# Second attention layer's keys: two batches prepared on VectorE alone in the layer before, two turned and split by GpSimd during the attention

## The chip, the cores and the metric

The kernel runs on one core of a Trainium2 chip. The metric is the device time in microseconds. Before the change three runs took 4261.15, 4261.16 and 4271.19 us, median 4261.16. The engines are named as in the profile: PE (TensorE), PEld (its weight loads), DVE (VectorE), ACT (ScalarE), POOL (GpSimd) and SP (SyncE, which here only issues DMAs).

## The reference

The network has four layers. Each adds a gated cross-attention and a gated feed-forward to x, [4 batches, 512 tokens, 256 features], float32. The context has 1601 rows of 256 features in each batch and is the same for all layers. The part that matters is the attention of the second layer, which turns (rotary position embedding) its queries and keys:

```python
q = (query @ Wq + bq).reshape(B, Sq, H, D)      # H = 16 heads, D = 16
k = (key @ Wk + bk).reshape(B, Sk, H, D)        # Sk = 1601
q = q * cq + _rotate_half(q) * sq_
k = k * ck + _rotate_half(k) * sk_
scores = einsum('bhqd,bkhd->bhqk', q, k) / sqrt(D)
scores = where(mask == 0, -1e+30, scores)
ctx = einsum('bhqk,bkhd->bqhd', softmax(scores), v).reshape(B, Sq, E)
```

In the first layer the attention is followed by a quantised linear map: x is layer-normalised, rotated by a Hadamard matrix, rounded to 4-bit levels and multiplied with a ternary weight.

## The kernel before

The stages run one after the other, with a fence between them: attention 1, quantised linear (926 to 1174 us of the span), attention 2 (1174 to about 2005 us), then experts, attention 3, experts, attention 4, experts. The context doesn't depend on x, so keys and values of an attention are prepared ahead, in the feed-forward stage in front of it, by the class `Prepared` and the functions `prepare_*`.

**Keys in parts.** In the first three attentions the scores are made of bfloat16 matmuls. A float32 key is split into three bfloat16 parts (`split3`, L873): part = value, rest = value - part, and so on. For the turned keys of attention 2 a piece (128 of the 256 key features x up to 512 of the 1601 context rows) goes through these steps in the quantised stage:

- PE makes the keys in PSUM (L267), ACT adds the bias and writes `p_kf` (L294).
- ACT issues two DMAs that copy `p_kf` with its two halves swapped into `p_kr` (L302).
- POOL or DVE does seven instructions (`prepare_split`, L335 to L337 and L876 to L879): p_kf x cosine, p_kr x sine, their sum, and the four of `split3`.
- SP stores the three parts to DRAM as `kready` (L239). ACT may overwrite a buffer of the ring of four only when this store has landed (the wait in front of L294).

Each of the four batches has the context chunks 512, 512, 512 and 65 rows wide. Two pieces a chunk make 32 pieces. With a chunk's keys PE also makes its values (L275), ACT copies them (L312) and stores them. The list in `quantised_linear` says which chunks belong to which of 11 parts and whether "pool", or "pool" and "dve" in turn, split them. The order of work is written by hand: `quant_pe`, `quant_act`, `quant_dve`, `quant_pool` place part by part between the layer norm "n", the four groups of tiles (`rotated`: x times the Hadamard matrix, L1603; `quantised` on DVE, L1550 to L1559; `xq` on POOL, L1505 and L1506; `product`, L1613 and L1622; the update of x on DVE, L1571) and the layer norm "c" (L95 to L145). Part 0 stands before norm "n", part 1 behind it, part 10 behind norm "c".

**Attention 2.** `Plan.lay_out_ready` writes a list of units that every engine runs through in order. `attend(g, b)` is one of 16 groups (four groups of four heads in four batches). It has 52 score steps `s2`, 0 to 51, and among them other units at steps given as (number, first, last): the row maxima of a later group (PE L1079, DVE L972, 988 ns each), then `peak` (DVE, six instructions on 128x16 numbers, L983 to L879), `turn` (PE L1085, DVE L991, then three DMAs `qaug<-tm`, L869, without which the next group's scores can't start), the softmax's `sum` and `norm`, and in `attend(0, b)` the two query pieces `q` of batch b+1, turned and split by POOL (L895 to L899 and L876 to L879). In `attend(1, b)` and later the `fetch` units load batch b+1's queries and keys (L844, L851) once the last scores of the old ones are done. SP issues its DMAs in the order of the units and waits in place.

PE runs through the same list. At the start of attention 2 SP issues weights, the table `turn`, the first keys, then after the two query pieces their fetch, output weights, values (L800), the keys of groups 1 to 3, and then the first `qaug<-tm` (L869).

## Time and profile before

| what | us |
|---|---|
| median of three runs | 4261.16 |
| the profiled execution, its own time | 4263.7 |
| its span, first to last instruction | 4262.5 |
| PE busy | 3602.4 (85%) |
| DVE busy | 2254.9 (53%) |
| ACT busy | 2084.6 (49%) |
| POOL busy | 641.6 (15%) |

The page gives for each group of instructions the busy time, the mean of one, and the idle time in front of it with what ended it. PE's weight loads overlap its matmuls. A granted clock of 1.00 is 2.4 GHz, of 0.50 is 1.2 GHz. The chain that ended last is only three pieces long here (12 us of the last expert stage), so it says nothing about the stages that are changed. They are read by windows and in order of time.

### The profile page before, as it was taken

The numbers are of one execution on the slowest core, as the hardware profiler recorded it, in microseconds if no ns is written. First come the engines' busy times: TensorE is split into PE (matmuls) and PEld (weight loads), VectorE is DVE, ScalarE is ACT, GpSimd is POOL, SyncE is SP. The second block draws the span as 40 slices with busy tenths as digits, with TensorE's granted clock in tenths as the row PEclk, the third lists the DMA queues.
The fourth block names the chain that finished last, engine by engine and source line by source line (L and its number), as shares of the span: only waits on it lengthen the run. The fifth ranks groups of instructions, "written<-read, shape, count | busy, mean of one in ns | idle before, by whom it ended". The sixth has DMA issues, their size and how long they took to land. (4 is left out here: it accounts for less than half of the span.)

```text
span 4262.5 us, 54212 instructions
## 1 busy us (share of the span) xinstructions
PE 3602.4 (85%) x19494; PEld 1931.4 (45%) x19494; DVE 2254.9 (53%) x3444; ACT 2084.6 (49%) x4574; POOL 641.6 (15%) x627
## 2 busy tenths in 40 slices
PE   3999999977649999998897699999989788794993
PEld 2334343335313333333695133333358556593993
DVE  4766666738747777773304677777630211342332
ACT  1566666652206666665233266666633322252662
POOL 1111111017711101001202101010011100003003
PEclk8999999988859999999898699999989899996996
DMA  6242424115452223212754633242055410203556
GB/s 131 43 67 46 63 46 63 16 55 163 138 118 38 56 39 61 34 17 92 221 177 148 115 42 59 34 68 32 1 186 202 154 76 31 89 23 113 185 184 100
DMA packets 231977, 375.68 MB, mean 88 GB/s; under 512 B 44528, under 2 KB 161896, under 8 KB 229664
## 3 DMA queue, kind: packets, MB, share of 16 engines
q1 hardware_dynamic: 188504, 240.83, 26.4%
q0 software_dynamic: 27360, 98.58, 7.7%
q10 hardware_dynamic: 15848, 32.80, 2.3%
q8 instruction: 159, 2.61, 0.3%
q14 instruction: 106, 0.87, 0.1%
HBM read 272.90 MB, written 91.40 MB: 85 GB/s over the span
## 5 line engine op out<-in xcount | busy, mean ns | idle before, releaser
L972 DVE TENSOR_REDUCE mxp<-m 128x1 f32<-128x802 f32 x1536 | 1447.1, 988 | 527.7 <-PE m L1079 525.1
L1190 ACT ACTIVATE e_t<-s 128x512 f32<-128x512 f32 (+1 forms) x2496 | 1355.5, 599 | 707.6 <-PE s L1098 706.5
L1079 PE MATMUL m<-kaug,qaug 97*128 97x401 bf16 x3072 | 812.6, 347 | 152.9 <-DMA qaug<-qready 57.8
L1098 PE MATMUL s<-qaug,kaug 100*128 100x512 bf16 (+1 forms) x2496 | 861.0, 384 | 28.6 <-DMA qaug<-tm 13.9
L1109 PE MATMUL pv<-e_t,v 128*32 128x512 f32 (+1 forms) x4992 | 667.4, 607 | 0.2
L1098 PEld LDWEIGHTS s<-qaug,kaug 100*128 100x128 bf16 (+1 forms) x2496 | 235.3, 101 | 698.5 <-ACT e_t L1190 489.3
L1079 PEld LDWEIGHTS m<-kaug,qaug 97*128 97x128 bf16 x3072 | 274.6, 99 | 555.1 <-DVE mxp L972 223.8
L2044 PE MATMUL y<-w,hT 128*128 (+1 forms) x1504 | 346.6, 384 | 11.7 <-DVE hT L1883 11.7
L2044 PEld LDWEIGHTS y<-w,hT 128*128 128x128 f32 x1504 | 283.2, 193 | 48.8 <-issue 6.4
L2035 PE MATMUL h<-xtT,w 128*128 128x128 f32 x2496 | 299.3, 279 | 6.8 <-DMA w<-in_L_w 3.3
L929 POOL TENSOR_TENSOR r<-ones,rc 128x512 f32<-128x512 f32 x48 | 49.9, 1039 | 1659.9 <-DVE rc L996 1659.9
L2035 PEld LDWEIGHTS h<-xtT,w 128*128 128x128 f32 x2496 | 292.6, 196 | 8.1 <-issue 7.4
L1888 DVE SCALAR_TENSOR_TENSOR y<-y,b 128x256 f32<-128x256 f32 x94 | 39.6, 421 | 328.0 <-PE y L2044 328.0
L2116 ACT ACTIVATE ez<-h,b 128x128 f32<-128x128 f32 x440 | 120.1, 388 | 158.9 <-PE h L2035 158.9
L1882 DVE TENSOR_SCALAR ez<-ez 128x1024 f32<-128x1024 f32 x55 | 38.2, 695 | 300.8 <-ACT z L2116 300.8
L1109 PEld LDWEIGHTS pv<-e_t,v 128*32 128x32 f32 (+1 forms) x4992 | 98.4, 108 | 216.6 <-ACT e_t L1190 151.5
L2121 ACT ACTIVATE hT<-h,b 128x128 f32<-128x128 f32 x312 | 84.9, 383 | 125.6 <-PE h L2035 125.5
L1839 POOL DMA_DIRECT2D w<-in_L_w x78 | 55.3, 708 | 505.5 <-PE h L2035 471.7
L2116 ACT ACTIVATE z<-h,b 128x128 f32<-128x128 f32 x440 | 122.8, 453 | 0.0
L267 PE MATMUL h<-p_ctx,p_wk 128*128 128x512 f32 (+1 forms) x256 | 105.7, 560 | 15.8 <-DMA p_ctx<-in_ctxT 14.7
L1358 PE MATMUL s<-kT,qT 128*128 128x512 f32 (+1 forms) x256 | 98.8, 541 | 19.4 <-ACT e_t L1413 15.3
L294 ACT ACTIVATE p_kf<-h,p_bk 128x512 f32<-128x512 f32 (+1 forms) x64 | 38.1, 595 | 142.9 <-PE h L267 111.0
(288 smaller groups left out, 3516.5 us busy)
## 6 DMA issues: line engine op xcount, KB each, us to landing
w<-in_L_w POOLq DMA_DIRECT2D x78, 1024.0 KB, 5.4
w<-in_L_w SPq DMA_DIRECT2D x24, 1024.0 KB, 13.3
kaug<-kready SPq DMA_DIRECT2D x192, 100.1 KB
kaug<-kready SPq DMA_DIRECT2D x96, 200.1 KB
p_ctx<-in_ctxT SPq DMA_DIRECT2D x36, 512.0 KB, 5.6
values<-p_vb ACTq DMA_DIRECT2D x36, 512.0 KB, 3.6
kready<-p_ks SPq DMA_DIRECT2D x48, 384.0 KB, 4.2
kaug<-kparts SPq DMA_DIRECT2D x84, 200.1 KB
```

The lines of the kernel that those rows point to most:

```text
L267: m = pe.matmul(p.slots[s % many][:, 0:n], p.wk[:, kc, P * j:P * j + P], p.at[:, f, kc, 0:n], start=kc == 0, stop=kc == DC - 1)
L972: dve.tensor_reduce(a.mxp[:, u.g % 2, half, n:n + 1], a.m_slot[u.m % 2][:].rearrange("p (a n) -> p a n", a=2)[:, :, 0:PIECE + 1], AX.XY, A ...
L1079: m = pe.matmul(slot[:, 512 * k:512 * k + PIECE + 1], a.qaug[0:R_MAX, u.g, j, P * qc:P * qc + P], a.kaug[0:R_MAX, u.g, j, k0:k0 + PIECE + ...
L1098: pe.matmul(slot[0:KW[u.k], :], a.kaug[0:R_ALL, u.g, u.j, P * u.k:P * u.k + KW[u.k]], a.qaug[0:R_ALL, u.g, u.j, :], start=True, stop=True) ...
L1109: m = pe.matmul(a.pv[32 * j:32 * j + 32, :], a.v[0:KW[u.k], u.k, u.g, VW * j:VW * j + 32], a.e_t[0:KW[u.k], u.n % 2, j, :], start=u.k == 0 ...
L1190: act.activation(a.e_t[0:KW[u.k], e % 2, u.j, :], a.s_slot[u.s % 3][0:KW[u.k], :], ACT.Exp).then_inc(s_free.sem, 1)
L1358: m = pe.matmul(a.s_ps[:, c0:c0 + w], a.qT[:, c, P * k:P * k + P], a.kT[:, b % 2, c, c0:c0 + w], start=c == 0, stop=c == DC - 1)
L1839: pool.dma_start(a.w1[:, m % 2, :, :], w["w1"][bass.ds(e, 1), :, :].rearrange("a (c p) f -> p (a c) f", p=P)).then_inc(wl[m % 2].sem, DMA)
L2035: m = pe.matmul(a.h_slot[i % 2][:, P * f:P * f + P], a.w1[:, w1_at, c, P * f:P * f + P], xT(c), start=c == 0, stop=c == DC - 1)
L2044: m = pe.matmul(a.y_slot[i % 2][:, 0:D], a.hT[:, i % 2, f, :], w2(f), start=f == 0, stop=f == FC - 1)
L2116: t = act.activation(to[:, p, P * f:P * f + P], slot[:, P * f:P * f + P], func, bias=bias(f))
L2121: t = act.activation(a.hT[:, p, f, :], slot[:, P * f:P * f + P], func, bias=bias(f))
```

## The change

1. In the quantised stage the batches are prepared in the order 2, 0, 3, 1. Only the pieces of batches 0 and 1 (`READY`) are turned and split there, all 16 by DVE. The pieces of batches 2 and 3 get no swapped copy and no split: ACT stores `p_kf` as float32 to DRAM `keys` (one DMA a piece). The parts have 1 chunk each (parts 0 to 8), then 3 and 4.
2. In attention 2, `attend(0, b)` to `attend(2, b)` for b = 0 and 1 carry eight `k` units of batch b+2. SP loads a piece's float32 keys and their swapped halves (three DMAs) while the piece before it is at work, POOL turns and splits it (seven instructions), SP stores it to `kready`.
3. SP issues the store of a piece one unit later than before (`store()`), and a table `turn_k` (128 x 3202 float32, 1.64 MB) is loaded at the start of attention 2 between the output bias and the values.

```diff
@@ Prepared
-                b, n_c = divmod(i, len(CHUNKS))
+                nth, n_c = divmod(i, len(CHUNKS))
+                b = order[nth]
-                    by = engines[k % len(engines)]
+                    by = engines[k % len(engines)] if b in in_parts else ""
@@ prepare_act
-            if p.rope is not None:
+            if x["by"] and p.rope is not None:
                 swapped = kn.sema(f"p_sw{f}", DMA)
...
-            if not p.in_parts:
+            if not x["by"]:
                 act.wait_ge(p_free.sem, p_free.at(s + 1))
                 act.dma_start(kn.dram["keys"][c["b"], P * j:P * j + P, c0:c0 + n], p.kf[:, f, 0:n]).then_inc(kept.sem, DMA)
@@ Plan.lay_out_ready
+            keys = [self.loaded(b + 2)] if self.rope and b + 2 < B and b + 2 not in READY else []
+            given = (len(CHUNKS) * DC // 4, 14, 48)
-            self.attend(0, b, peaks, *last, *queries)
+            self.attend(0, b, peaks, *last, *queries, *((k, *given) for k in keys))
...
-                self.attend(g, b, peaks, *renew, (self.normalise(g - 1, b), 2, 2 * HG, JOBS - 1))
+                self.attend(g, b, peaks, *renew, *((k, *given) for k in keys), (self.normalise(g - 1, b), 2, 2 * HG, JOBS - 1))
@@ head_ready_sp
+    def store():
+        if held:
+            x = held.pop()
+            sp.wait_ge(split[x.by].sem, split[x.by].at(x.n + 1))
+            sp.dma_start(to[x.b, ...], a.split_at[x.f][2][:, :, 0:n]).then_inc(stored[x.f].sem, DMA)
+    def load(x):
+        src = kn.dram["keys"][x.b, P * x.j:P * x.j + P, c0:c0 + n]
+        sp.dma_start(kf[:, 0:n], src).then_inc(arrived.sem, DMA)
+        for r in (0, P // 2):
+            sp.dma_start(kr[r:r + P // 2, 0:n], src[P // 2 - r:P - r, :]).then_inc(arrived.sem, DMA)
+                sp.dma_start(a.turn_k[:], a.rope[1]).then_inc(tables_k.sem, DMA)
-        elif u.kind == "q":
-            sp.wait_ge(split[u.by].sem, split[u.by].at(u.n + 1))
-            sp.dma_start(queries[u.b, ...], ...)
+        elif u.kind in ("q", "k"):
+            store()
+            held.append(u)
+            after = splits[splits.index(u) + 1:][0:1]
+            for x in after:
+                if x.kind == "k":
+                    load(x)
@@ quantised_linear
-        both = ("pool", "dve")
-        a.p = Prepared(..., True, rope,
-                       ((1, ("pool",)), (1, ("pool",)), *((1, both) for _ in range(7)), (4, both), (3, both)))
+        a.p = Prepared(..., (2, 0, 3, 1), READY, rope,
+                       (*((1, ("dve",)) for _ in range(9)), (3, ("dve",)), (4, ("dve",))))
@@ quant_pool
-    split(0)
-    split(1)
...
-    for part in (7, 8, 9):
-        split(part)
     norm_pool(kn, "c")
-    split(10)
```

Three places of the new order matter. The first is DVE in the quantised stage, behind an update of x (L1571 before, L1614 now). Before, one piece follows (L335 to L879), because POOL has the chunk's other piece:

```order
L1571 SCALAR_TENSOR_TENSOR x<-y_81,gates,x 128x512
L1571 SCALAR_TENSOR_TENSOR x<-y_82,gates,x 128x512
L335 TENSOR_TENSOR p_kf<-p_kf,p_turn 128x512
L336 TENSOR_TENSOR p_kr<-p_kr,p_turn 128x512
L337 TENSOR_TENSOR p_kf<-p_kf,p_kr 128x512
L876 TENSOR_TENSOR p_ks<-p_kf,ones 128x512
L877 TENSOR_TENSOR p_kr<-p_kf,p_ks 128x512
L878 TENSOR_TENSOR p_ks<-p_kr,ones 128x512
L879 TENSOR_TENSOR p_ks<-p_kr,p_ks 128x512
L95 BN_STATS stats<-x 128x6 x4
```

Now both pieces of the chunk follow on DVE (L340 to L927 are the same seven instructions):

```order
L1614 SCALAR_TENSOR_TENSOR x<-y_81,gates,x 128x512
L1614 SCALAR_TENSOR_TENSOR x<-y_82,gates,x 128x512
L340 TENSOR_TENSOR p_kf<-p_kf,p_turn 128x512
L341 TENSOR_TENSOR p_kr<-p_kr,p_turn 128x512
L342 TENSOR_TENSOR p_kf<-p_kf,p_kr 128x512
L924 TENSOR_TENSOR p_ks<-p_kf,ones 128x512
L925 TENSOR_TENSOR p_kr<-p_kf,p_ks 128x512
L926 TENSOR_TENSOR p_ks<-p_kr,ones 128x512
L927 TENSOR_TENSOR p_ks<-p_kr,p_ks 128x512
L340 TENSOR_TENSOR p_kf<-p_kf,p_turn 128x512
L341 TENSOR_TENSOR p_kr<-p_kr,p_turn 128x512
L342 TENSOR_TENSOR p_kf<-p_kf,p_kr 128x512
```

DVE's row got longer there, while POOL keeps only L1556 and L1557 (the old L1505 and L1506) in the whole stage. The second place is SP in `attend(0, 0)` of attention 2, between the next values (vn) and the DMAs of the turn (qaug<-tm). Before:

```order
L800 DMA vn<-values 128x3072 [waits v_taken]
L801 DMA vn<-values 65x256
L827 DMA qready<-ks 128x3x512 [waits split_pool] x2
L869 DMA qaug<-tm 1x16x128 [waits m_free]
L869 DMA qaug<-tm 1x16x128 x2
L844 DMA qaug<-qready 16x4x512 [waits s_full,stored1,stored0]
```

Now, with the loads of the float32 keys (kf and kr from keys) and the stores that wait for POOL:

```order
L842 DMA vn<-values 128x3072 [waits v_taken]
L843 DMA vn<-values 65x256
L826 DMA qready<-ks 128x3x512 [waits split_pool]
L835 DMA kf<-keys 128x512
L837 DMA kr<-keys 64x512 x2
L826 DMA qready<-ks 128x3x512 [waits split_pool]
L835 DMA kf<-keys 128x512
L837 DMA kr<-keys 64x512 x2
L826 DMA kready<-ks 128x3x512 [waits split_pool]
L835 DMA kf<-keys 128x512
L837 DMA kr<-keys 64x512 x2
L917 DMA qaug<-tm 1x16x128 [waits m_free]
```

One store that waits for POOL's first key piece, and three loads, now stand in front of the turn's DMAs. The third place is POOL at the end of `attend(0, 0)`. Before, nothing follows the two query pieces (kf, kr and ks at set 1 are the last) but the reciprocals' spreading (r<-ones,rc) of the later groups:

```order
L876 TENSOR_TENSOR ks<-kf,ones 128x512 [waits stored1,pool_own]
L877 TENSOR_TENSOR kr<-kf,ks 128x512 [waits pool_own]
L878 TENSOR_TENSOR ks<-kr,ones 128x512 [waits pool_own]
L879 TENSOR_TENSOR ks<-kr,ks 128x512 [waits pool_own]
L929 TENSOR_TENSOR r<-ones,rc 128x512 [waits m_free]
L929 TENSOR_TENSOR r<-ones,rc 128x512 [waits m_full,m_free] x3
```

Now three key pieces stand there (the third is shown), then r, then three more in the next group:

```order
L950 TENSOR_TENSOR kf<-kf,turn_k 128x512 [waits tables_k,kl0]
L951 TENSOR_TENSOR kr<-kr,turn_k 128x512
L952 TENSOR_TENSOR kf<-kf,kr 128x512 [waits pool_own]
L924 TENSOR_TENSOR ks<-kf,ones 128x512 [waits stored0,pool_own]
L925 TENSOR_TENSOR kr<-kf,ks 128x512 [waits pool_own]
L926 TENSOR_TENSOR ks<-kr,ones 128x512 [waits pool_own]
L927 TENSOR_TENSOR ks<-kr,ks 128x512 [waits pool_own]
L984 TENSOR_TENSOR r<-ones,rc 128x512 [waits m_free]
L950 TENSOR_TENSOR kf<-kf,turn_k 128x512 [waits tables_k,kl1]
```

By the whole list, groups 0, 1 and 2 of batches 0 and 1 get three, three and two (65 wide) key pieces. PE's and ACT's instructions are the same in kind and number but for ACT's DMA issues.

## Rows read from the trace of the kernel before

**Rows 1.** Windows: us; busy PE, PEld, DVE, ACT, POOL; granted clock; DMA share; GB/s.

```profile
926.40:1173.60 247.20, 163.60 (x564) 104.59 (x564) 199.31 (x257) 61.21 (x134) 169.57 (x137) 0.83 0.51 153
...
1322.70:1364.80 42.10, 40.06 (x241) 13.66 (x245) 32.33 (x43) 29.20 (x54) 1.04 (x1) 1.00 0.30 40
1449.00:1505.10 56.10, 53.98 (x289) 22.69 (x285) 36.50 (x50) 32.23 (x59) 19.46 (x17) 1.00 0.34 74
```

**Rows 2.** Groups by line, 926.4 to 1173.6: busy, mean ns | idle before, releasers.

```profile
L294 ACT ACTIVATE p_kf<-p,p_bk 128x512 f32<-128x512 f32 (+1 forms) x32 | 19.0, 595 | 107.8 <-PE p L267 67.5 <-DMA kready<-p_ks 39.0 <-PE p L275 1.2
```

**Rows 3.** DVE in order of time: start us, us, operation, [idle before <-releaser].

```profile
945.04 14.56 DVE L122 TENSOR_SCALAR xq<-x,mv,rstd 128x256 f32<-128x256 f32 x12 [7.26 <-PE t L135]
...
989.33 2.84 DVE L336 TENSOR_TENSOR p_kr<-p_kr,p_turn 128x512 f32<-128x512 f32 x1
...
1028.16 1.19 DVE L1550 TENSOR_REDUCE sc<-xh 128x4 f32<-128x1024 f32 x1
...
1035.72 0.68 DVE L335 TENSOR_TENSOR p_kf<-p_kf,p_turn 128x512 f32<-128x512 f32 x1
...
1132.94 5.75 DVE L122 TENSOR_SCALAR xq<-x,mv,rstd 128x256 f32<-128x256 f32 x16 [3.02 <-POOL rstd L113]
...
1169.34 0.35 DVE L879 TENSOR_TENSOR p_ks<-p_kr,p_ks 128x65 bf16<-128x65 f32 x1
...
1187.71 0.69 DVE L899 TENSOR_TENSOR kf<-kf,live 128x512 f32<-128x512 f32 x1
```

**Rows 4.** POOL in order of time, quantised stage.

```profile
1145.41 1.26 POOL L335 TENSOR_TENSOR p_kf<-p_kf,p_turn 128x512 f32<-128x512 f32 x1 [12.50 <-DMA p_kr<-p_kf]
...
1173.60 1.43 POOL L910 MEMSET fill<- 4x1601 bf16 x1 [3.98 <-DMA kready<-p_ks]
```

**Rows 5.** PE in order of time, quantised stage.

```profile
960.80 6.10 PE L267 MATMUL p<-p_ctx,p_wk 128*128 128x512 f32 x8 [0.46 <-ACT xnT L145]
...
977.30 3.60 PE L267 MATMUL p<-p_ctx,p_wk 128*128 128x512 f32 x8
...
1016.94 3.72 PE L1603 MATMUL h<-hd,xc 128*128 128x256 f32 x16 [1.93 <-ACT xc L1657]
1020.50 3.60 PE L267 MATMUL p<-p_ctx,p_wk 128*128 128x512 f32 x8
...
1028.59 1.04 PE L1613 MATMUL t<-ident,xq 128*128 128x128 f32 x8
...
1033.76 3.60 PE L267 MATMUL p<-p_ctx,p_wk 128*128 128x512 f32 x8
...
1139.65 3.70 PE L267 MATMUL p<-p_ctx,p_wk 128*128 128x512 f32 x8 [0.46 <-ACT xnT L145]
```

**Rows 6.** PE, first scores of attention 2.

```profile
1270.24 0.61 PE L1098 MATMUL s<-qaug,kaug 100*128 100x512 bf16 x1 [13.95 <-DMA qaug<-tm]
```

**Rows 7.** DMA, GB/s in 40 slices of 1200 to 1250.

```profile
GB/s 118 197 45 184 120 107 126 101 125 101 125 104 132 116 336 485 403 433 140 61 67 77 79 69 77 77 69 69 85 72 77 74 82 79 85 82 85 90 85 90
```

**Rows 8.** POOL, pieces of the next batch's queries, attention 2.

```profile
1461.89 1.28 POOL L895 TENSOR_TENSOR kf<-kf,turn 128x512 f32<-128x512 f32 x1 [2.93 <-ACT kr L1160]
...
1480.10 1.15 POOL L879 TENSOR_TENSOR ks<-kr,ks 128x512 bf16<-128x512 f32 x1
```

**Rows 9.** DVE, a peak beside POOL in attention 1.

```profile
213.75 0.24 DVE L983 TENSOR_TENSOR mx<-mxp 128x16 f32<-128x16 f32 x1
...
214.24 1.01 DVE L876 TENSOR_TENSOR nm<-mx,ones 128x16 bf16<-128x16 f32 x1
```

**Rows 10.** POOL at that place.

```profile
214.04 1.18 POOL L879 TENSOR_TENSOR ks<-kr,ks 128x512 bf16<-128x512 f32 x1
```

**Rows 11.** DVE in attention 2: attend(1, 0), then attend(0, 1).

```profile
1354.00 0.17 DVE L983 TENSOR_TENSOR mx<-mxp 128x16 f32<-128x16 f32 x1
...
1471.47 2.79 DVE L972 TENSOR_REDUCE mxp<-m 128x1 f32<-128x802 f32 x3 [0.64 <-PE m L1079]
...
1492.53 0.17 DVE L983 TENSOR_TENSOR mx<-mxp 128x16 f32<-128x16 f32 x1
```

More of the change, by code:

```diff
@@ L420, in add @@
         if kind in ("q", "k"):
-            u.s = self.next("s", 2 if self.rope else 1)
+            if kind == "q" or not self.ready:
+                u.s = self.next("s", 2 if self.rope else 1)
             u.n = self.next("split_" + u.by)
+            if kind == "k" and self.ready:
+                u.at = self.next(f"kl{u.f}")
             u.before = self.set_of.get(u.f)
@@ L580, in lay_out_ready, with loaded @@
                 pass
+    def loaded(self, b):
+        for n_c in range(len(CHUNKS)):
+            for c in range(DC):
+                self.split("k", b, c, n_c, ("pool",))
+                yield
     def renew(self, g, b):
@@ L811, in head_ready_sp @@
             if rope:
[L812 removed]
+                sp.dma_start(a.turn[:], a.rope[0][:, :, 0:T]).then_inc(tables.sem, DMA)
                 n_of("tables")
@@ L833, in head_ready_sp @@
             if "q" in u.what:
+                store()
                 for f in range(2):
-                    sp.wait_ge(stored[f].sem, stored[f].at(u.b + 1))
+                    last = max(n for (_, b, *_), (at, n) in a.stored_of.items() if b == u.b and at == f)
+                    sp.wait_ge(stored[f].sem, stored[f].at(last))
             if u.b:
@@ L1728, in experts @@
         if ahead:
-            a.p = Prepared(kn, sb, ahead, [s[:, 512 * i:512 * i + 512] for s in a.h_slot for i in range(2)], kind == "relu", None,
+            a.p = Prepared(kn, sb, ahead, [s[:, 512 * i:512 * i + 512] for s in a.h_slot for i in range(2)], range(B),
+                           range(B) if kind == "relu" else (), None,
                            ((2, ("pool",)), (5, ("dve",)), (5, ("dve",)), (4, ("dve",))))
```

70 lines of the change are left out of this document (42 added, 28 removed).

## The prediction

> **What bounds the kernel now.** I read windows first. In the quantised stage (926.4 to 1173.6, 247.2 us) no engine is full by its mean: DVE 199.3 busy, POOL 169.6, PE 163.6 [rows 1]. In attention 2 PE is full: 40.06 of 42.10 us in a plain group, 53.98 of 56.10 in the group that also makes queries, with the clock at its upper level, 2.4 GHz; POOL is busy for 1.04 and 19.46 [rows 1]. So the change takes work from a stage where DVE and POOL are both loaded, and gives it to an engine that idles beside a full PE.
>
> Then the groups by line: the ring of four buffers is what holds the quantised stage. ACT sits 39.0 us in front of L294 until a store `kready` lands, thus until a split is done [rows 2], and PE's value matmuls queue behind ACT. In order of time one sees why the splits are slow. A 128x512 instruction takes DVE 0.69 us when POOL is silent and up to 2.84 when both run [rows 3]. DVE's twelve normalising instructions of norm "n" take 14.56 us beside POOL's splits, where the sixteen of norm "c" take 5.75 [rows 3]. Two engines splitting side by side need about 11 us for two pieces; DVE alone needs 7 x 0.72 = 5.05 a piece (0.69 and the gap), so 10.1 for two. POOL gives the stage nothing.
>
> Here the Trainium skill (SBUF — State Buffer, "SBUF: two separate sides") has a rule: DVE and GpSimd share a port pair as an exclusive lock, and the second to start waits for the whole instruction of the first; a DVE operation takes part if it has two SBUF inputs or a two-port mode. The trace agrees: DVE's tiny L876 starts at 214.24 and ends at 215.25, where POOL's instruction ends at 215.22 [rows 9, 10]. The rule speaks for the first half of the change and against the second; I weigh that below.
>
> **Quantised stage, step by step.**
> (a) Norm "n": POOL no longer splits beside it. Twelve instructions at norm "c"'s rate are 4.3 us instead of 14.56 [rows 3]: **-10**.
> (b) From PE's second chunk (960.80) to the end of norm "c" (1139.65), 178.9 us [rows 5]. PE's blocks without stalls: start with weight transposes and first rotation 16.5 (960.80 to 977.30); a chunk 8.1 (1020.50 to 1028.59), seven of them 56.7; a 65-wide chunk an estimated 2.6 (an eighth of the key columns and a quarter of the value tiles of 8.1, and round trips), three of them 7.8; a rotation 1.93 + 3.56 = 5.5, three 16.5; a product 5.2 (1028.59 to 1033.76), four 20.8; norm "c" 6.2 (5.75 and its lag). Sum 124.5 [rows 3, 5]. What stays: DVE works in the third group of tiles 7.6 on the levels (1028.16 to 1035.72 [rows 3]), 10.1 + 10.1 on four pieces, 4 that POOL's two `xq` instructions still take from it, 3 on updates and statistics, 35 in all, against PE's 27 there; the batch 3 chunk behind it then waits for the ring about 3 us and the last product for POOL's `xq` about 4. I add 2 for a first wait and 5 for stretches at the lower level of the clock (eight matmuls 6.10 instead of 3.60 [rows 5]; the stage's mean is 0.83). 138.5: **-40**.
> (c) Tail behind norm "c": before, 1139.65 to 1173.60, 33.95 us [rows 4, 5], with two big and one small piece on each engine. Now batch 1 is whole there: 5.8 to the first swapped copy (1139.65 to 1145.41), six pieces of 5.05, two small ones of 7 x 0.25 to 0.35 (about 2 each), 4.0 for the last store (1169.69 to 1173.60 [rows 3, 4]): 44, so **+9**.
> ACT's new stores of float32 keys replace two DMA issues by one; they land in a few us, less than any split took, and hide behind PE. Stage: -41. Bounds: -52 with no rest in (b), -29 if the clock stays low for most of the stage.
>
> **Start of attention 2.** `turn_k`, 1.64 MB, is put in front of the values and of three groups' keys in SP's queue. The first `qaug<-tm` already lands late: PE waits 13.95 us for it with nothing else open [rows 6], behind those transfers. The values' 1.6 MB took four slices of 1.25 us at 336 to 485 GB/s [rows 7], so 4 us later lands 4 us later: **+4**. Bounds: 0 (if it fits into slices now at 70 to 90 GB/s) and 8 (at 200 GB/s).
>
> The Trainium skill (DMA: Bandwidth & Descriptors, "Queues, rings and completion order") says that each DMA engine consumes the descriptors of a ring in order but that completion isn't first-in-first-out across engines. By order alone the cost is the +4; if the little DMAs could pass, it would be near 0.
>
> **In the groups of attention 2.** Per batch POOL gets six pieces of 8.5 us (a query piece is 9.7, half of 1461.89 to 1481.25 [rows 8], less one instruction) and two small ones of 2.2. PE and ACT have the same instructions. POOL's 55 us a batch lie beside PE. SP: in `attend(0, b)` the turn's DMAs now stand behind the store of the first key piece, which POOL ends at 1481.25 + 8.5 = 1489.8; the peak before that turn starts at 1492.53 [rows 11], so SP is free, 3 us ahead. In `attend(1, b)` SP is free after fetch, load and one store, over 10 us ahead. Keys of batch 2 are wanted a whole batch (190 us) after they are split. The row maxima read PSUM: beside POOL's query pieces three take 2.79 us [rows 11], 0.93 each, not slowed. Nothing there.
>
> What isn't free is the peak: six dependent DVE instructions on 128x16 numbers in SBUF, 0.2 us each, for which PE waits in line. POOL's second key piece runs 1489.8 to 1498.3, over the peak at 1492.53 [rows 8, 11]; the same holds in `attend(0, 0)`. In `attend(1, b)` three pieces, 25.5 us of POOL, share 42 us; the first can start behind the sum, the other two wait for loads queued behind the fetch, and by my estimate run over the peak, 31 us into the group (1354.00 in the one from 1322.7 [rows 1, 11]). Four peaks. The one case in this trace: the peak at 213.75 in attention 1 meets the end of a POOL instruction (L983 0.24) and a second one of 1.18; L876 takes 1.01 instead of 0.17 [rows 9, 10]. That one cost 0.9 us, two DVE instructions having slipped in between two of POOL's. With POOL busy throughout, three of six are held by some 0.85: 2.5 a peak, **+10**. Bounds: 0.9 a peak, 4; six held by 1.0 each, 6 a peak, 24. Small additions to x that meet POOL: **+1** (0 to 3).
>
> By the rule on the shared port each DVE instruction could be blocked for a whole POOL instruction: that is the upper bound, 24 instead of 10, and the fourth rival below.
>
> **Sum.** -41 + 4 + 10 + 1 = -26 against the profiled execution's own 4263.7 (span 4262.5 and 1.2 around it), thus 4237.7. The median of the runs, 4261.2, is 2.5 below that execution: I forecast **4235 us**. Its own range is 4225 to 4245.
>
> **The rivals.**
> 1. The peaks aren't hit, or what PE loses there it makes up: -36, 4225. For it: the case of rows 9 cost under 1 us. Against: here POOL runs 36 us without a break. With the quantised stage at its best it goes to 4214.
> 2. The quantised stage isn't held by splits but by PE with its clock and by ACT's round trips: it gives 25, the rest as above, 4251; no change that can be told. For it: 163.6 of 247.2 is PE's, at a mean of 0.83 [rows 1]. Against: the 39.0 us in front of L294 [rows 2].
> 3. Slower: the row maxima can't run beside POOL after all, over the long run. POOL's 2 x 55 = 110 us are then lost to DVE, whose idle time is 9.8 in a plain group (42.10 - 32.33 [rows 1]), 59 in six. 51 reach PE: -41 + 4 + 51 = +14, 4275. It decides from the point where over 37 us of the 110 come through. Against: 2.79 for three.
> 4. Every peak instruction is blocked: +24 instead of +10, 4249.
>
> **How the numbers follow.** Forecast 0.45; rival 1 0.22; rival 2 0.13; rival 4 0.12; rival 3 0.05; some stall I didn't see 0.03. A measurement of this kernel tells 0.3%, 12.8 us, from nothing: faster means under 4248.4. Forecast and rival 1 lie there whole, of rivals 2 and 4 some two fifths: faster 0.77, same 0.16, slower 0.07. The range leaves out 0.2: 4214 to 4257.
>
> **What would show it.** Right: the quantised stage lasts about 206 us, DVE's split instructions take 0.69, L122 of norm "n" 0.36 each, ACT's wait for `kready` falls from 39.0 to under 10; POOL's instructions there number about ten; `qaug<-tm` ends PE's wait about 4 us later, counted from the stage's start; plain groups without key pieces keep 42.1, `attend(0, b)` and `attend(1, b)` for b = 0 and 1 are 2 to 3 us longer, and L876 to L879 on 128x16 numbers show 1 us. Wrong: the quantised stage over 220 us; L972 above 1.05; PE waiting for `qaug<-tm` at the head of later groups because SP stood at a store.

## The result

The changed kernel takes 4218.94 us (median of 4 runs, 4213.84 to 4220.32) against 4261.99 of the kernel before in the same measurement; the ratio is 0.9883, with a 95% interval of 0.9865 to 0.9901. Two later measurements on other chips gave 0.9896 (0.9875 to 0.9917) and 0.9897 (0.9881 to 0.9914). The forecast was 4235, with a range of 4214 to 4257: the direction is right; the gain is 43 us by the medians (50 by the ratio; 44 by the two later ratios) where 26 were forecast.

The profiled execution took 4219.2 us, its span 4218.0, which is 44.5 less than before. Everything behind attention 2 is as long as it was, so the 44.5 lie in two stages: the quantised stage and attention 2. Below, each piece of the prediction's sum with its landmarks (start of the stage, PE's second chunk, first chunk behind norm "c", GpSimd's memset, first score, start of the next stage's norm):

| piece | before | after | difference | forecast |
|---|---|---|---|---|
| (a) up to PE's second chunk | 960.80 | 949.52 | -11.3 | -10 |
| (b) middle, to the end of norm "c" | 178.85 | 131.24 | -47.6 | -40 |
| (c) tail | 33.95 | 40.66 | +6.7 | +9 |
| start of attention 2, to the first score | 96.64 | 88.38 | -8.3 | +4 |
| all groups of attention 2 | | | +15.9 | +11 |
| sum | | | -44.5 | -26 |

### The profile page after: what moved, and what is told of

It reads as the page before. It is cut to its first block and busy times, and to the rows that moved or that the text cites. A ratio compares the mean times of both kernels' runs of the same rounds, so it can differ in the third digit from the quotient of the medians.

```text
span 4218.0 us, 54261 instructions
## 1 busy us (share of the span) xinstructions
PE 3591.1 (85%) x19494; PEld 1923.1 (46%) x19494; DVE 2201.1 (52%) x3458; ACT 2080.0 (49%) x4574; POOL 602.2 (14%) x613
## 3 DMA queue, kind: packets, MB, share of 16 engines
q1 hardware_dynamic: 193512, 249.03, 27.3%
## 5 line engine op out<-in xcount | busy, mean ns | idle before, releaser
L1027 DVE TENSOR_REDUCE mxp<-m 128x1 f32<-128x802 f32 x1536 | 1447.2, 987 | 524.2 <-PE m L1134 521.6
L984 POOL TENSOR_TENSOR r<-ones,rc 128x512 f32<-128x512 f32 x48 | 49.9, 1039 | 1519.9 <-DVE rc L1051 1519.9
L280 PE MATMUL h<-p_wv,p_ctx 128*128 128x256 f32 (+1 forms) x416 | 102.3, 396 | 18.1 <-issue 5.9
L1413 PE MATMUL s<-kT,qT 128*128 128x512 f32 (+1 forms) x256 | 99.9, 546 | 20.8 <-ACT e_t L1468 15.3
```

The source lines that it names most:

```text
L280: m = pe.matmul(p.slots[s % many][0:KW[t], 0:D], p.at[:, f, kc, k0:k0 + KW[t]], p.wv[:, kc, :], start=kc == 0, stop=kc == DC - 1)
L1027: dve.tensor_reduce(a.mxp[:, u.g % 2, half, n:n + 1], a.m_slot[u.m % 2][:].rearrange("p (a n) -> p a n", a=2)[:, :, 0:PIECE + 1], AX.XY, A ...
L1413: m = pe.matmul(a.s_ps[:, c0:c0 + w], a.qT[:, c, P * k:P * k + P], a.kT[:, b % 2, c, c0:c0 + w], start=c == 0, stop=c == DC - 1)
```

## The profile after

Windows of the quantised stage in the profile after, one for each of (a), (b), (c); columns as in [rows 1].

```profile
933.50:949.52 16.02, 13.43 (x56) 8.38 (x56) 5.45 (x17) 7.41 (x22) 2.90 (x1) 0.85 0.92 322
949.52:1080.76 131.24, 110.07 (x425) 76.62 (x425) 92.65 (x165) 43.03 (x91) 22.44 (x9) 0.93 0.50 155
1080.76:1121.42 40.66, 24.66 (x84) 14.66 (x84) 30.91 (x56) 9.29 (x21) 0.00 (x0) 0.85 0.46 142
```

From here on the quantised stage is counted from GpSimd's first instruction of norm "n" (933.46 before, 933.50 after) to its memset: 187.9 us instead of 240.1. Counted from 926.4, as in the prediction, it is 195.0 instead of 247.2, where the prediction expected about 206. VectorE has 129.0 us of work in it; GpSimd, busy for 169.6 us before [rows 1], has 25.3 in ten instructions. In the middle PE works 110 of 131 us.

ACT's group of that stage, then VectorE in order of time: norm "n", and the first pieces of the tail.

```profile
L299 ACT ACTIVATE p_kf<-p,p_bk 128x512 f32<-128x512 f32 (+1 forms) x32 | 19.0, 595 | 85.2 <-PE p L272 68.2 <-issue 10.2 <-DMA kready<-p_ks 3.7
```

```profile
944.35 1.38 DVE L122 TENSOR_SCALAR xq<-x,mv,rstd 128x256 f32<-128x256 f32 x4 [6.52 <-PE t L135]
945.89 2.68 DVE L122 TENSOR_SCALAR xq<-x,mv,rstd 128x256 f32<-128x256 f32 x8 [0.17 <-PE t L135]
...
1086.54 0.69 DVE L340 TENSOR_TENSOR p_kf<-p_kf,p_turn 128x512 f32<-128x512 f32 x1 [6.74 <-DMA p_kr<-p_kf]
1087.15 0.68 DVE L341 TENSOR_TENSOR p_kr<-p_kr,p_turn 128x512 f32<-128x512 f32 x1
```

The 39.0 us of waiting for `kready` in front of L294 [rows 2] are 3.7 in front of L299 (the same line). Norm "n" writes its tiles at 0.34 us each, where the twelve took 14.56 [rows 3]. In the tail a split instruction takes 0.69.

PE in the middle: the start block, the two products with waits and a low clock, then a chunk that isn't split and, from the tail, the value matmuls of one that is.

```profile
949.52 3.70 PE L272 MATMUL p<-p_ctx,p_wk 128*128 128x512 f32 x8 [0.46 <-ACT xnT L145]
...
1033.42 5.41 PE L1665 MATMUL y<-wqT,xqT 128*128 128x256 f32 x16 [2.29 <-ACT xqT L1717]
...
1048.96 1.09 PE L1656 MATMUL t<-ident,xq 128*128 128x128 f32 x8 [3.07 <-POOL xq L1557]
1052.19 6.51 PE L1665 MATMUL y<-wqT,xqT 128*128 128x256 f32 x16 [2.13 <-DVE x L1614]
...
1058.54 3.60 PE L272 MATMUL p<-p_ctx,p_wk 128*128 128x512 f32 x8
1061.97 3.80 PE L280 MATMUL p<-p_wv,p_ctx 128*128 128x256 f32 x16
...
1092.39 1.03 PE L280 MATMUL p<-p_wv,p_ctx 128*128 128x256 f32 x4
1093.59 1.13 PE L280 MATMUL p<-p_wv,p_ctx 128*128 128x256 f32 x4 [0.17 <-ACT p_kf L299]
1095.21 1.99 PE L280 MATMUL p<-p_wv,p_ctx 128*128 128x256 f32 x8 [0.48 <-ACT p_vb L317]
```

A chunk whose pieces aren't split takes PE 7.07 us (1058.54 to 1065.61), one that is split 8.1, as before [rows 5]. For the first ACT issues one DMA a piece (0.33 us), for the second two (1.16 us), and there the value matmuls wait for ACT.

PE at the first score of attention 2, and what the DMAs moved between the memset and that place, in 40 slices of 1121.42 to 1222:

```profile
1209.80 0.61 PE L1153 MATMUL s<-qaug,kaug 100*128 100x512 bf16 x1 [8.16 <-DMA qaug<-tm]
```

```profile
GB/s 114 220 116 52 76 92 113 118 204 35 156 119 125 133 133 132 276 420 433 395 116 97 103 116 107 117 118 120 117 121 124 190 167 170 223 165 6 0 0 0
```

PE waits 8.16 us for `qaug<-tm`, not 13.95 [rows 6]. The values and the table are there, four slices of 2.5 us at 276 to 433 GB/s; but the keys of groups 1 to 3 behind them drain at 97 to 124 GB/s, where they drained at 61 to 90 [rows 7].

A peak beside GpSimd, in `attend(1, 0)`: VectorE, GpSimd and PE in order of time.

```profile
1296.87 1.06 DVE L1038 TENSOR_TENSOR mx<-mxp 128x16 f32<-128x16 f32 x1
1297.96 0.18 DVE L1039 TENSOR_SCALAR mx<-mx 128x16 f32<-128x16 f32 x1
1298.17 0.89 DVE L924 TENSOR_TENSOR nm<-mx,ones 128x16 bf16<-128x16 f32 x1
1299.10 0.17 DVE L925 TENSOR_TENSOR mx<-mx,nm 128x16 f32<-128x16 f32 x1
1299.31 1.01 DVE L926 TENSOR_TENSOR nm<-mx,ones 128x16 bf16<-128x16 f32 x1
1300.36 0.18 DVE L927 TENSOR_TENSOR nm<-mx,nm 128x16 bf16<-128x16 f32 x1
```

```profile
1296.63 1.26 POOL L952 TENSOR_TENSOR kf<-kf,kr 128x512 f32<-128x512 f32 x1
1297.97 1.06 POOL L924 TENSOR_TENSOR ks<-kf,ones 128x512 bf16<-128x512 f32 x1
1299.11 1.18 POOL L925 TENSOR_TENSOR kr<-kf,ks 128x512 f32<-128x512 f32 x1
```

```profile
1300.68 0.27 PE L1140 MATMUL m<-identb,nm 128*128 128x128 bf16 x1 [3.33 <-DVE nm L927]
```

Every second instruction of the chain of six is held, and ends when GpSimd's does: 1.06, 0.89, 1.01 us instead of 0.17. This is the prediction's picture. The like happens at exactly four peaks (1252.35, 1296.87, 1439.83, 1486.89), where three, three, two and four of the six are held and PE stands for 3.11, 3.33, 2.96 and 4.38 us. In the kernel before PE stands for 1.23, 0.88, 0.76 and 0.88 us at these places. The row maxima beside it are not slower (L1027, 987 ns a piece in the whole kernel). But there is one thing more, in windows around that peak:

```profile
1296.00:1300.00 4.00, 1.35 (x11) 0.21 (x3) 3.83 (x6) 1.57 (x3) 3.77 (x4) 1.00 0.01 2
1300.00:1304.00 4.00, 3.32 (x13) 0.71 (x14) 1.72 (x4) 0.60 (x1) 3.84 (x5) 0.57 0.02 3
1304.00:1308.00 4.00, 4.00 (x24) 1.45 (x22) 2.68 (x3) 3.19 (x7) 3.77 (x4) 1.00 0.43 115
```

As the stall ends the granted clock falls, to a mean of 0.57 over four microseconds: PE runs at its lower level, 1.2 GHz, and needs 1.88 us for the eight `pv` matmuls that took 1.06 just before the stall.

## The experiments: groups of attention 2

Group lengths are read between two starts of GpSimd's `r` (L984, one in each group). Before: 42.1, or 56.1 with queries; after: 45.92 and 47.01 for `attend(1, b)`, 59.94 for `attend(0, 1)`; `attend(0, 0)`, from its first score, 64.75 instead of 61.44.

**e3_tiny.**

```diff
     if a.ready and u.kind == "k":
+        n = 8
+        src, o = kf[:, 0:n], kr[:, 0:n]
```

> The changed kernel, in which GpSimd's seven instructions of a key piece work on 8 columns instead of 512 (batches 2 and 3 get keys that are not split whole); all DMAs, waits and their order stay. This takes the time on GpSimd away and leaves the traffic. Theory of the prediction (the shared port at the peaks): the four longer groups go back to 61.4, 42.1, 56.1 and 42.1, the whole is 16 us less than the changed kernel, 4203. Rival (the loads and stores on SP's queue lengthen the groups): nothing changes, 4219.

Ratio 0.9860 (0.9840 to 0.9880), 4197.97 us. Groups: 61.2, 42.11, 56.12, 42.08; the loads (three DMAs) and the store of each piece are all still there.

```profile
1270.88:1312.99 42.11, 40.04 (x239) 13.64 (x237) 32.24 (x41) 29.38 (x55) 5.12 (x23) 1.00 0.56 95
```

The 16 us come from GpSimd's time at work, not from the DMAs of its pieces. Its keys of batches 2 and 3 stay unsplit but for 8 columns, so this kernel only serves to tell the two apart.

**e2_placed.**

```diff
-            self.attend(0, b, peaks, *last, *queries, *((k, *given) for k in keys))
+            self.attend(0, b, peaks, *last, *queries)
-  self.attend(g, b, peaks, *renew, *((k, *given) for k in keys), (self.normalise(...), ...))
+  self.attend(g, b, peaks, *renew, (self.normalise(...), ...), *((k, (0, 2, 2, 4)[g], 9, 12) for k in keys))
```

> The changed kernel with GpSimd's key pieces placed otherwise: none in attend(0, b), and 2, 2 and 4 in attend(1, b) to attend(3, b), each lot directly behind the sum of its group, so that it should end before the group's peak. Theory of the prediction (only the peak pays): the four groups that were 3.3, 3.8, 3.8 and 4.9 us longer go back to 61.4, 42.1, 56.1 and 42.1, none other grows by over 0.5, and the whole falls by 16 us against the changed kernel, to 4203. Rival (GpSimd's pieces cost DVE and thereby PE something wherever they stand): the same 16 us turn up in other groups, 4219. Second rival (the loads of float32 keys collide with the renewals' fetches): groups grow at their heads, where PE waits for DMA.

Ratio 1.0030 (1.0018 to 1.0041), slower than the kernel before. My edit was not what I meant: `attend` goes on past `last`, so all eight pieces came into `attend(1, b)`. Those two groups took 76.91 and 78.18 us, all others 42.08 and 56.10. PE there:

```profile
1300.03 0.27 PE L1139 MATMUL m<-identb,nm 128*128 128x128 bf16 x1 [4.07 <-DVE nm L926]
...
1337.73 0.61 PE L1152 MATMUL s<-qaug,kaug 100*128 100x512 bf16 x1 [25.76 <-DMA qaug<-tm]
```

The peak itself cost 4.07, but SyncE then stood at the stores of the pieces while GpSimd split them one by one (it ended the last at 1338), with the peak's three little DMAs queued behind. By accident this prices a queue in which the turn's DMAs stand behind stores that wait for six more pieces: PE waits 25.76 us for `qaug<-tm` the first time and 26.94 the second. The prediction had worked out one such store as free in the changed kernel, and there no group shows such a wait.

**e7_spread.**

```diff
+                some = (0, 2, 2, 4)[g]
+                turned = [(self.some(keys[0], some), some, 2 * HG + 1, 2 * HG + 8)] if keys else []
```

> What the first placement was meant to be: GpSimd's key pieces behind each group's sum, two in attend(1, b), two in attend(2, b), four (two of them small) in attend(3, b), none in attend(0, b); all else as in the changed kernel. (The first placement gave all eight to attend(1, b), and those groups took 76.9 and 78.2 us.) Theory (only the peak pays, and a store for which SP stands in front of a peak's DMAs): two pieces end 18.1 us behind the start of the sum, the peak comes at 22.3; all groups of attention 2 keep 42.1 and 56.1, the first 61.4; 16 us less than the changed kernel, 4203. Rival (pieces cost something wherever they stand): a group with two pieces is 1 to 4 us longer, 4210 to 4219.

Ratio 0.9906 (0.9891 to 0.9921), 4222.86 us. Groups with two pieces: 45.74, 48.56, 45.18, 46.15; those with four: 42.29, 42.29. Neither theory as written: the second piece was late. GpSimd in `attend(1, 0)` and PE's windows for `attend(1, 0)` to `attend(3, 0)`:

```profile
1279.96 1.28 POOL L956 TENSOR_TENSOR kf<-kf,turn_k 128x512 f32<-128x512 f32 x1
...
1295.86 1.27 POOL L956 TENSOR_TENSOR kf<-kf,turn_k 128x512 f32<-128x512 f32 x1 [7.51 <-DMA kr<-keys]
```

```profile
1278.96:1324.70 45.74, 41.68 (x239) 13.92 (x237) 34.26 (x41) 29.57 (x55) 17.03 (x16) 0.96 0.45 76
1324.70:1373.26 48.56, 44.51 (x239) 14.38 (x237) 34.43 (x41) 29.64 (x55) 17.05 (x16) 0.89 0.44 74
1373.26:1415.55 42.29, 40.04 (x238) 13.63 (x236) 32.44 (x41) 29.28 (x54) 21.22 (x30) 1.00 0.41 75
```

Its load stands behind the renewal's fetch in SyncE's queue and comes 7.51 us late (6.7 to 8.8 in the four groups with two pieces), so that the piece lies on the peak at 1301.28. The group of 48.56 has the same stall (2.99 us) as that of 45.74 (2.91), but the clock stays down for longer (mean 0.89 against 0.96); the 2.8 us between the two are the clock's alone. Around the stall of the longer one:

```profile
1324.70:1350.00 25.30, 21.93 (x129) 7.20 (x126) 20.38 (x24) 16.93 (x31) 15.76 (x14) 1.00 0.60 91
1350.00:1355.00 5.00, 4.50 (x16) 1.17 (x17) 1.53 (x4) 1.29 (x3) 1.29 (x2) 0.50 0.22 71
1355.00:1360.00 5.00, 5.00 (x18) 1.24 (x16) 1.99 (x2) 2.18 (x4) 0.00 (x0) 0.50 0.04 12
1360.00:1365.00 5.00, 5.00 (x31) 1.52 (x29) 4.51 (x5) 3.71 (x7) 0.00 (x0) 0.97 0.00 0
```

Four pieces cost 0.2 us where the big ones' loads came in time.

**e9_ahead.** As e7_spread, and the next two pieces' loads go ahead of the fetch:

```diff
             if "q" in u.what:
                 store()
+                for x in splits[ahead:ahead + 2]:
+                    if x.kind == "q":
+                        break
+                    load(x)
```

> The spread placement (2, 2 and 4 key pieces behind the sums of attend(1, b) to attend(3, b)), with the float32 keys of a group's first two pieces loaded ahead of the renewal's fetch instead of behind it. In the spread placement the second piece waited 7.5 to 8.8 us for its load, ran over the peak at 22.3 us behind the sum, and the groups were 3.1 to 6.5 us longer, part of it with PE's clock at half. Theory (only what is stalled at the peak costs, and the low clock that follows the stall): two pieces end 18 us behind the sum, every peak is free but for the small pieces of attend(3, b), the clock stays at its upper level, groups keep 42.1, 56.1 and (first) 61.4; 14 to 16 us less than the changed kernel. Rival (GpSimd's pieces or their transfers cost something wherever they stand): groups remain 1 us or more longer.

Ratio 0.9857 (0.9833 to 0.9881), 4194.21 us. Groups 61.2, 42.07, 42.08, 42.24, 56.12, 42.07, 42.08, 42.30. Windows of `attend(1, 0)` to `attend(3, 0)`, VectorE at the peak, PE behind it:

```profile
1273.38:1315.45 42.07, 40.04 (x239) 13.64 (x237) 32.22 (x41) 29.38 (x55) 16.93 (x15) 1.00 0.50 85
...
1357.53:1399.77 42.24, 40.04 (x238) 13.63 (x236) 32.38 (x41) 29.29 (x54) 21.18 (x30) 1.00 0.34 63
```

```profile
1295.69 0.17 DVE L1055 TENSOR_TENSOR mx<-mxp 128x16 f32<-128x16 f32 x1
...
1296.11 0.18 DVE L941 TENSOR_TENSOR nm<-mx,ones 128x16 bf16<-128x16 f32 x1
```

```profile
1297.06 0.22 PE L1157 MATMUL m<-identb,nm 128*128 128x128 bf16 x1 [0.87 <-DVE nm L944]
```

GpSimd does all its 17 to 21 us of pieces in each of these groups, and nothing is lost: at the peak PE waits 0.87 us, and the clock stays at 1.00. In these groups a piece on GpSimd costs only where it lies on the chain of small VectorE instructions. The ratio's interval overlaps that of the changed kernel; what shows the gain are the group lengths.

## The experiments: the quantised stage

**e4_all_dve.** `READY = (0, 1, 2, 3)`, with the first two chunks' splits placed ahead of the first group of tiles.

> The changed kernel, but VectorE alone splits the keys of all four batches in the quantised stage (batch order 2, 0, 3, 1 kept), and GpSimd splits no keys in attention 2. It tells what stopping GpSimd gives by itself from what moving half the pieces gives. Theory of the prediction (GpSimd gave the stage nothing; DVE alone takes 5.05 us a piece): between PE's second chunk and the end of norm c DVE then has 18 big pieces x 5.05 + 6 small x 2 = 103 us, levels, updates and statistics 42, weights 12, together 157 instead of 131.2, so the stage is about 26 us longer than the changed kernel's, 214; attention 2 loses the 16 us at the peaks; 4219 + 26 - 16 = 4229. Rival (what counts is that half the pieces are gone, two engines share the rest as well as one): the stage takes its old 240 to 247 us, 4219 + 56 - 16 = 4259.

Ratio 0.9994 (0.9979 to 1.0009). The stage takes 229.7 us, 16 more than my theory, 10 less than the kernel before; and the stretch to the first score is 104.4, which neither had. The middle is 171.9 us instead of the 157 that I had worked out as VectorE's work: the last six pieces of batch 3 stand in front of norm "c", where PE waits for VectorE:

```profile
1114.73 1.08 PE L135 MATMUL t<-ident,xq 128*128 128x128 f32 x4 [16.70 <-DVE xq L122]
```

Part (a) is 17.1 us here and 27.3 before: GpSimd's silence gives it with all pieces still there.

**q1_both.** The engines `("pool", "dve")` by turns in the changed kernel's plan, with GpSimd's `split(part)` calls as before.

> The changed kernel, in which GpSimd and VectorE share the 16 pieces of batches 0 and 1 in the quantised stage by turns, as in the kernel before; the 16 pieces of batches 2 and 3 stay in attention 2. The fourth corner of the square: both engines and 32 pieces 240.1 us, VectorE alone and 32 pieces 229.7, VectorE alone and 16 pieces 187.9. Theory (GpSimd's help is worth nothing): by turns two pieces take 11 us instead of 10.1, norm n has no splits beside it either way, so the stage is 0 to 10 us longer than 187.9 and the whole the same to 10 us more than the changed kernel, 4218 to 4228. Rival (with few pieces left GpSimd takes real load from VectorE): the stage falls under 183.

Ratio 0.9894 (0.9874 to 0.9913), the changed kernel's own value. The stage takes 191.4 us; nine other executions that split the 16 pieces on VectorE alone have 185.6 to 190.8. So the square is:

| stage, us | 32 pieces | 16 pieces |
|---|---|---|
| both engines | 240.1 (three other profiles 242 to 244) | 191.4 |
| VectorE alone | 229.7 | 187.9 |

By these single profiles GpSimd's silence gives 10 us with 32 pieces, all of it in (a), 27.3 to 17.1, while the middle gives back the 7 us that the tail costs; and 3.5 with 16 pieces, where neither kernel has splits beside norm "n"; q1_both is only 0.6 us above the longest of the nine. The moved pieces give 42 to 49. The prediction was right that GpSimd gave the stage nothing. Of the moved pieces' 69 us on VectorE (12 x 5.05 and 4 x 2) the stage gives back 42, of which about 4 are PE's shorter chunks; that the rest had lain beside PE is argued, not measured.

**e11_tail.** e9_ahead, the fastest kernel here, with the batches in the order `(2, 0, 1, 3)`.

> The kernel with keys loaded ahead of the fetch (the best so far, 0.9857), with the batches prepared in the order 2, 0, 1, 3, so that the last batch, behind norm c, has no pieces to split. The tail behind norm c was 40.7 us, with 34 us of VectorE's splits; without them its four chunks are PE's 27 and about 4 around them. The six big and two small pieces are 34 us more for VectorE between PE's second chunk and norm c, where it is busy for 92.7 of 131.3 us. If the slack takes them: stage 8 to 12 us shorter, whole 4184 to 4188. If they come where the three chunks in front of norm c stand together, the middle grows by as much as the tail shrinks: no difference.

Ratio 0.9870 (0.9853 to 0.9887), no better than e9_ahead. The tail falls from 40.7 to 26.0 us, but the stage is 193.8 instead of 190.8: in front of norm "c" PE now waits 17.60 us for VectorE. The new tail is gained and lost again in front of norm "c": the second case of the expectation, here 3 us worse.

## The experiments: the start of attention 2

The stretch is the time from the memset to the first score.

**b1_alloc.** The kernel before, with `turn_k` allocated and unused.

> The kernel before with nothing but the 12.5 KB per partition of the keys' table set aside in attention 2, which moves all later SBUF tensors of that stage, the buffers of augmented keys and queries among them; nothing is loaded into it. Layout theory (where the keys' buffer lies decides how fast its fetches drain): the stretch after the values' load runs at 95 to 131 GB/s as in the changed kernel, not at 67 to 90; PE's wait for the first peak's DMAs falls from 13.95 to under 4 and the whole by 10 to 14 us, 4249. Rival (the drain depends on what is in DRAM, on the order of the stores, or on nothing that the allocation moves): 13.95 stays, 4261.

Ratio 1.0002 (0.9991 to 1.0013); 99.9 us, wait 17.37, slices from 65 to 84 GB/s. Where the buffers lie isn't the cause.

**b3_order.** The kernel before, with `b = (2, 0, 3, 1)[b]` in the preparation.

> The kernel before with one thing of the change: the batches are prepared in the order 2, 0, 3, 1 instead of 0, 1, 2, 3; both engines split all of them as before. The fetches of groups 1 to 3 of batch 0 drained at 65 to 95 GB/s in the kernel before and with its buffers moved, and at 95 to 138 in all four kernels with the change. If it is the order (which batch's keys were written when), the fetches run at over 95 here too, PE's wait of 13.95 us for the first peak's DMAs falls below 4, and the whole is 10 to 14 us less, 4247. If it isn't the order but what GpSimd or the reloaded keys do, 65 to 95 GB/s and 4260 stay.

Ratio 1.0004 (0.9992 to 1.0015); 96.0 us, wait 13.79. Nor is the order.

**b2_load.** The kernel before, with `turn_k` allocated and loaded ahead of the values.

> The kernel before with nothing but the load of the keys' table (1.64 MB) put where the change puts it, unused. It measures the prediction's term for the start of attention 2 alone. Theory of the prediction (the bytes are ahead of the first peak's DMAs in an ordered queue): +4, from the stage's end to the first score about 101 to 104 us, where three runs without it show 96.0, 96.6 and 99.9. Rival (fitted in at no cost): 96 to 100.

Ratio 1.0015 (0.9998 to 1.0032); 98.1 us. Three profiles without the load have 96.0 to 99.9: by this one the +4 can't be seen. Over its twelve runs the ratio is some 0.0012 above those of b1_alloc and b3_order, about 5 us, which isn't clear of the noise either.

**e1_turn_late.** The changed kernel with the load of `turn_k` behind the first peak's DMAs.

> The changed kernel with one DMA moved: the table of rotations for the keys (1.64 MB) is issued behind the DMAs of the first peak instead of ahead of the values and of three groups' keys. Theory of the prediction (the queue is drained in order, so the table's bytes are paid once by the first peak's DMAs): from the quantised stage's end to attention 2's first score 88.4 us becomes about 84, PE's wait there 8.16 becomes about 4, the whole 4 us less than the changed kernel (4219 to 4215). Rival (the table fits in where the queue is slow, it costs nothing): 88.4 stays, 4219. Either way the stretch stays far below the 96.6 of the kernel before, since something else made the keys' fetches drain faster.

Ratio 0.9879 (0.9859 to 0.9898). 81.7 us, PE finding `qaug<-tm` landed; keys at 92 to 138 GB/s.

**e10_ahead_late.** e9_ahead with the load placed as in e1_turn_late.

> The same as the kernel with keys loaded ahead of the fetch, and the keys' table loaded behind the first peak's DMAs instead of ahead of the values. Theory (in order through the queue, the table costs the first peak's DMAs 4 to 9 us): from the quantised stage's end to the first score 82 us as in the run with the table alone moved (1117.23 to 1198.91), against 88 to 96 in five runs with the table in front; the whole 20 to 25 us less than the changed kernel, about 4195. Rival (the 82 was a run with a fast fetch by chance): 88 to 96.

Ratio 0.9861 (0.9838 to 0.9884), nothing gained on e9_ahead: 93.9 us, with the keys at 82 to 103 GB/s. So the 81.7 was mostly a fast fetch, and single executions of one program differ here:

**c_after** and **c2_after**, the changed kernel unchanged.

> The changed kernel as it is, on the same chip as the other runs of this set, to compare them with it. The first measurement gave 0.9883 of the kernel before. Expected: the same ratio within 0.002, the quantised stage about 188 us, 88 us from its end to attention 2's first score, and four groups longer by 3.3, 3.8, 3.8 and 4.9 us.

Ratio 0.9896; stage 187.3, stretch 92.8; groups 65.77, 45.95, 61.05, 43.83. In the last of them PE stands at the peak for 2.62 us, but no low clock follows; the group is longer by the stall alone. In the 61.05 the clock stays low for twice as long as in the profile above.

> The changed kernel again, on the chip of the other runs of this set. It gives a third value for the stretch from the quantised stage's end to the first score, which was 88.4 and 92.8 us in two executions: 88 to 96 expected, so that a difference of under 5 us in this stretch between single profiles says little. The whole 0.988 to 0.990 of the kernel before, and 10 to 16 us more than the kernel with keys loaded ahead.

Ratio 0.9897; stretch 92.1. The stretch in all profiles so far, by what stands in front of the first peak's DMAs and by the pieces that the stage ahead splits and stores:

| stretch, us | 32 pieces | 16 pieces |
|---|---|---|
| no table in front | 96.0, 96.6, 99.9 (mean 97.5) | 81.7, 93.9 (mean 87.8) |
| table in front | 98.1, 104.4 (mean 101.2) | nine, 87.9 to 95.8 (mean 91.1) |

Down the columns the table costs 3.7 and 3.3 us on average, near the forecast's +4, though no pair of profiles could show it and three of the four means rest on two or three profiles. Along the rows 16 pieces instead of 32 are 10 us less. In the kernels of the right column the stage ahead writes less to DRAM (4.9 MB of split keys less, 3.3 MB of float32 keys more), and it makes half as many swapped copies. The next two runs add writes alone:

**x1_stores.** 16 more stores, 4.9 MB, at the end of the changed kernel's quantised stage.

```diff
+    for b in (2, 3):
+        for j in range(DC):
+            for c0, n in CHUNKS:
+                sp.dma_start(kn.dram["kready"][b, :, P * j:P * j + P, c0:c0 + n].rearrange("a p k -> p a k"),
+                             a.p.ks[:, j, :, 0:n]).then_inc(kn.sema("again", DMA).sem, DMA)
```

> The changed kernel with 16 more stores at the end of the quantised stage, which write 4.9 MB of split keys (of no meaning; they are overwritten before they are read) to the places of batches 2 and 3. In all kernels in which the split keys of all four batches were written in that stage (five runs) the fetches of groups 1 to 3 of batch 0 drained at 65 to 95 GB/s, in those where only batches 0 and 1 were written (six runs) at 74 to 138. If the writes make later reads slow, the fetch drains at 65 to 80 here, and the first score comes over 100 us behind the stage's end. If not, 80 to 130 GB/s and 88 to 96 us. The stage itself is 20 to 30 us longer in either case.

Ratio 0.9992 (0.9979 to 1.0006); stage 208.8, stretch 99.5.

**x3_spare.** The same stores to a buffer `spare` that nothing reads.

> As the run with 16 more stores at the end of the quantised stage, but into a buffer of DRAM of their own that nothing reads, not into batches 2 and 3 of the split keys. That run's fetches drained at 69 to 97 GB/s, and its first score came 99.5 us behind the stage's end. If it was the place that was written, the fetch is as in the changed kernel's family here (80 to 130 GB/s, 88 to 96 us). If it was the amount written shortly before, or chance, 69 to 97 GB/s and about 99 again.

Ratio 0.9972 (0.9958 to 0.9985); stretch 108.0. What the DMAs moved in 1145.73 to 1253.73, in 40 slices, and PE's first score:

```profile
GB/s 121 245 55 50 103 132 158 58 143 0 146 165 125 122 127 172 418 445 423 116 69 71 75 74 69 70 70 74 71 94 126 109 115 150 85 75 74 74 79 166
```

```profile
1253.76 0.61 PE L1153 MATMUL s<-qaug,kaug 100*128 100x512 bf16 x1 [26.17 <-DMA qaug<-tm]
```

The keys drain at 69 to 75 GB/s for nine slices, though these stores go elsewhere: it isn't the place. Both runs with more written have a longer stretch than all eleven profiles of the right column, the longest of which has 95.8. The other runs of the two kernels point the same way. By the ratios they take about 43 and 34 us more than the changed kernel (0.9992 and 0.9972 against 0.9892, the mean of its three), while the stage is 21 and 25 us longer in the profiles; by this estimate some 20 and 10 are left for what follows. That more written makes the stretch longer fits all 18 profiles, within each row of the table with 2 us to spare. It isn't in proportion to the amount (1.6 MB more in the left column for 10 us, 4.9 MB in a burst at the stage's end here for 8 and 17 against the mean of 91.1), and by what mechanism it acts stays open.

## Why the prediction was right in direction and wrong in size

**(a) Norm "n"**: forecast -10, measured -11.3. Right, by the mechanism named; e4_all_dve has it too.

**(b) The middle**: forecast -40, measured -47.6. The mis-sized term is the sum of PE's blocks, 124.5, and not the 14 added for waits and clock. Read without waits and low clock, the blocks of the profile after come to about 117. The start block was read as 16.5 from a place where eight matmuls took 6.10 us at the lower clock; they take 3.70 now, and the block 13.4. A chunk was priced at 8.1, but the four that aren't split take 7.07. The prediction had seen that ACT issues fewer DMAs for them and gave it no term; this is 4 us. Waits and low clock are the rest, some 14 us, as forecast in sum but not in kind: none for the ring at PE (3 forecast; 3.7 us in the whole stage, on ACT), 3.07 for `xq` (4 forecast), 3.3 for two products that wait for `xqT` and x, and 7.9 in which three blocks of 16 matmuls take 5.41 and one 6.51 us instead of 3.72. (The clock's mean in the middle is 0.93, where it was 0.86.) That the sum of the 14 was right is in part luck.

**(c) The tail**: forecast +9, measured +6.7. The terms listed add up to 44.1, which is 10 more than 33.95 and not 9. Pieces are 4.84 us apart, not 5.05 (1.3 us in all), small ones take 1.6, not 2 (0.7), and the last store 2.6, not 4.0 (1.4).

**The start of attention 2**: forecast +4, measured -8.3. This step failed in sign, and it is the largest single miss, 12 us. The step that failed is that the fetch of groups 1 to 3 would drain as before, so that only the table's bytes would be added in front of `qaug<-tm`. The load itself was priced about right as far as can be told: +3.7 and +3.3 by the means of the table above, within a spread as large. What I put at nothing is a gain of about 10 us: the fetch of keys behind the table drains at 97 to 124 GB/s instead of 61 to 90. It goes with less being written in the stage ahead; the mechanism stays open. No row of the trace before shows it, since there the fetch has but one speed. (The profiled execution, at 88.4, lies 3 us under the mean of its kind.)

The Trainium skill (DMA: Bandwidth & Descriptors, "Queues, rings and completion order") has the descriptors of a ring consumed in order. The means of 3.7 and 3.3 us lie near the 4 that come from it; with two profiles that differ by 12 us among them they don't exclude the 0 of little DMAs that pass.

**The groups**: forecast +10 at four peaks, +1 elsewhere; measured +15.9 at those four and 0 elsewhere. The stall itself was sized right: 3.11, 3.33, 2.96, 4.38 against 1.23, 0.88, 0.76, 0.88 before, about 2.5 more each, 10 in all. The step that failed here is that a stall costs only its own length. Missing was the low clock behind each stall, the rest of the 15.9: 1.4 to 1.6 us a peak, 6 in all. e7_spread shows it by itself: like stalls, 45.74 and 48.56 us. So does c_after: a stall without low clock, 43.83 us.

The Trainium skill (SBUF — State Buffer, "SBUF: two separate sides") says that the second engine to start waits for the whole instruction of the first. The rows agree, each held instruction ending with GpSimd's; but as a rule one of VectorE's slips in between two of GpSimd's, so two to four of six are held. Rival 4, with all six, is out.

**The rivals.** 1 (peaks free): no, though e9_ahead makes it true. Its numbers (4225, and 4214 with the stage at its best) lie nearest to the measured 4218.94, but by luck: the peaks cost 16 us, and the stage and the start gave more. 2 (stage bound by PE, 25 us): no, the stage gave 52, but PE and the waits around it do bound what is left. 3 (row maxima blocked): no, 987 ns.

The net error of 18.5 us is 11 too little gained in the stage and 12 at the start, and 5 the other way in the groups, so part of the misses cancel. The measured time lies below the 4225 to 4245 that the forecast claimed for its own mechanism.

## What to carry to other kernels

When work is moved to an engine that shares a port with another, list the other's short dependent chains on the critical path, and place the work between them; put its loads ahead of bulk transfers in the queue, or the placement is lost. Here this gave about 0.3% more (0.9857 against 0.9883 to 0.9897; by the group lengths the 16 us that the change's placement lost). When a wait is removed, remove with it the low clock that came from it; when a stall is added, add the clock that it may cost. Read the length of a block where the clock is at the level that it will have, and where the other engines do what they will do.
